# Selective scan: every B product through a transpose, four of them as a matmul with a diagonal of B, sums as transposes, softplus in three ScalarE steps

## What is computed

```
x_dbl = einsum('bkdl,kcd->bkcl', xs, x_proj_weight);  dts, Bs, Cs = split(x_dbl)
delta = softplus(einsum('bkrl,kdr->bkdl', dts, dt_projs_weight) + dt_projs_bias)
def step(h, (u, d, B, C)):
    h = exp(d[..., None] * A) * h + d[..., None] * B[:, :, None, :] * u[..., None]
    y = sum(h * C[:, :, None, :], axis=-1)
out_y = ys + xs * Ds;   y = out_y of the four directions, turned back and added
```

## Time and profile before

| | |
|---|---|
| median of 3 launches | 27518.19 us (27503.76 to 27527.82) |
| the profiled execution | 27545.74 us, span of its core 27544.1 us |
| busy over the span | PE 92%, DVE 85%, ACT 77%, POOL 77% |
| granted TensorE clock, mean | 0.945 |
| bytes moved by DMA | 1243.41 MB, mean 45 GB/s |

### The profile page before, as it was taken

The page is one execution under the profiler, slowest core; times in us unless marked ns, Lnnn a source line. Parts: engine busy times, 40 slices in busy tenths (PEclk is TensorE's granted clock), DMA queues, the critical chain, the costliest instruction groups (busy, mean ns, idle before and its releaser), DMA issues. The chain is left out here.

```text
span 27544.1 us, 304787 instructions
## 1 busy us (share of the span) xinstructions
PE 25272.9 (92%) x87136; PEld 12653.6 (46%) x87136; DVE 23277.2 (85%) x22864; ACT 21119.5 (77%) x39912; POOL 21115.4 (77%) x9545
## 2 busy tenths in 40 slices
PE   7999889998799988999889998899988999889998
PEld 3455444554345544455434554445544455444554
DVE  6799867998679986799867998679986799867998
ACT  4799747997479974799757996579964799747997
POOL 3799737997379973799737997379973799737997
PEclk8999989999899998999989999899998999989999
DMA  0122101221012210122101221012210122101221
GB/s 8 46 64 63 45 8 46 63 63 45 9 46 63 63 45 8 46 63 63 45 8 47 63 63 45 8 48 63 63 46 6 47 63 63 44 8 46 64 63 45
DMA packets 796846, 1243.41 MB, mean 45 GB/s; under 512 B 220800, under 2 KB 238080, under 8 KB 792064
## 3 DMA queue, kind: packets, MB, share of 16 engines
q1 hardware_dynamic: 795136, 1223.32, 15.1%
HBM read 1155.89 MB, written 67.11 MB: 44 GB/s over the span
## 5 line engine op out<-in xcount | busy, mean ns | idle before, releaser
L1590 PE MATMUL ps<-arena,ident 128*128 128x512 f32 x24576 | 11420.8, 596 | 2.8 <-DVE arena L1425 1.8
L1413 DVE TENSOR_TENSOR_SCAN arena<-arena,ps 128x512 f32<-128x512 f32 x7680 | 9250.5, 1259 | 120.2 <-ACT arena L1776 62.7
L1966 POOL TENSOR_TENSOR arena<-arena 128x1536 f32<-128x1536 f32 x1920 | 6636.8, 3462 | 84.6 <-ACT arena L1796 83.8
L1787 ACT ACTIVATE scaled<-arena,cols 128x384 f32<-128x384 f32 x10240 | 5807.5, 606 | 695.8 <-PE ps L1559 695.8
L1590 PEld LDWEIGHTS ps<-arena,ident 128*128 128x128 f32 x24576 | 4350.6, 190 | 4319.9 <-issue 4013.6
L1413 DVE TENSOR_TENSOR_SCAN arena<-ps,arena 128x512 f32<-128x512 f32 x4608 | 5576.4, 1260 | 74.8 <-ACT ps L1776 74.7
L1956 POOL TENSOR_TENSOR arena<-arena 128x1536 f32<-128x1536 f32 x1536 | 5311.3, 3467 | 326.5 <-DVE arena L1413 325.4
L1776 ACT ACTIVATE arena<-arena 128x512 f32<-128x512 f32 x7680 | 5240.8, 713 | 11.6 <-PE ps L1590 11.6
L1559 PEld LDWEIGHTS ps<-ident,scaled 128*128 128x128 f32 x30720 | 3537.4, 141 | 1987.1 <-issue 1173.7
L1559 PE MATMUL ps<-ident,scaled 128*128 128x128 f32 x30720 | 4195.7, 276 | 139.0 <-ACT scaled L1787 60.7
L1776 ACT ACTIVATE ps<-arena 128x512 f32<-128x512 f32 x4608 | 3125.1, 683 | 64.0 <-DVE arena L1413 25.1
(11 more groups left out here) (190 smaller groups left out, 32155.8 us busy)
## 6 DMA issues: line engine op xcount, KB each, us to landing
arena<-rows SPq DMA_DIRECT2D x3456, 256.0 KB, 3.2
spare<-rows SPq DMA_DIRECT2D x640, 256.0 KB, 3.3
arena<-x SPq DMA_DIRECT2D x16, 1536.0 KB, 13.4
x<-arena SPq DMA_DIRECT2D x16, 1536.0 KB, 10.7
arena<-x SPq DMA_DIRECT2D x64, 384.0 KB, 8.0
out<-arena SPq DMA_DIRECT2D x64, 384.0 KB, 3.0
rows<-xd SPq DMA_DIRECT2D x256, 64.0 KB, 2.7
arena<-L_conv_fc_w SPq DMA_DIRECT2D x16, 576.0 KB, 5.3
```

Of the source, the lines that this page charges most:

```text
L1413: nc.vector.tensor_tensor_scan(flip(states(b, n, t)), flip(decays), flip(adds), carry[:, k, N2 * n + t:N2 * n + t + 1], ALU.mult, ALU.add) ...
L1590: nc.tensor.matmul(m.ps[:, t, :], m.ident[:, :], states(b, n, t), start=False, stop=(n == SUMS[t][-1])).then_inc(at[Y_MM[t]], 1)
L1787: nc.scalar.activation(scaled[:, j, :], turned[:, j, :], ACT.Copy, scale=b_cols[:, b % 2, j, n:n + 1]).then_inc(at["scaled_out"], 1)
L1966: nc.gpsimd.tensor_tensor(out, out, each, ALU.mult).then_inc(at["hp_ready"], 1)
```

## The change

The six plain states go away: all 16 products come by TensorE. For twelve (`SCALED`) the pieces are scaled as before, but 13 of the 48 pieces of a block are scaled on GpSimd (`POOL_PIECES`); there are two buffers of `scaled` and two of `turned`. For four (`DIAGONAL` = 3, 6, 11, 15) ScalarE scales the 128x128 identity by the column of B, and `turn_back` is a real matmul of `turned` with it. VectorE multiplies by C only for states 4, 9 and 15, GpSimd for thirteen. `add_up` becomes four transposes that accumulate, so y arises with tokens on partitions; `lift_y` copies it to SBUF, `turn_y` transposes it back, and the older y is added there. The bias of delta enters as a thirteenth row of the matmul. The softplus is Abs, Exp, Ln(1+x) on ScalarE; VectorE has `rounded` ((w+1)-1, from SBUF to SBUF) and `above` (max(x,0)+l, from PSUM); GpSimd's three steps stay. The weights of the projection are kept for two directions at a time and loaded again during the scan; the DMAs of B's rows go.

```diff
-POOL_C = (0, 1, 3, 4, 6, 7, 9, 11, 12, 13)
-TURNED = (1, 2, 4, 5, 7, 8, 10, 11, 13, 14)
+POOL_C = (0, 1, 2, 3, 5, 6, 7, 8, 10, 11, 12, 13, 14)
+DIAGONAL = (3, 6, 11, 15)
+POOL_PIECES = {1: (2, 3), 2: (3,), 4: (2, 3), 7: (2, 3), 8: (3,), 10: (2, 3), 13: (2, 3), 14: (3,)}
...
-                nc.vector.scalar_tensor_tensor(sp_e, sp_w, 1.0, m.ps[:, AH, :], ALU.subtract,
-                                               ALU.subtract).then_inc(at["sp_dve"], 1)
+                nc.vector.tensor_scalar(sp_e, sp_w, 1.0, 1.0, ALU.add, ALU.subtract).then_inc(at["sp_dve"], 1)
+            def above(b, t):
+                dve.wait_ge(at["sp_act"], 3 * u + 3)
+                nc.vector.scalar_tensor_tensor(delta[:, b % 2, t, :], m.ps[:, AH, :], 0.0, sp_l, ALU.max,
+                                               ALU.add).then_inc(at["sp_dve"], 1)
...
+                if n in DIAGONAL:
+                    for j in range(N4):
+                        ins = nc.tensor.matmul(bank(b, n, t)[:, j * 128:(j + 1) * 128], turned[b % 2][:, j, t * 128:(t + 1) * 128],
+                                               diagonals[no % 2][:, j, :], start=True, stop=True)
...
-                nc.tensor.matmul(m.ps[:, t, :], m.ident[:, :], states(b, n, t), start=False,
-                                 stop=(n == SUMS[t][-1])).then_inc(at[Y_MM[t]], 1)
+                for j in range(N4):
+                    ins = nc.tensor.matmul(m.ps[:, t, j * 128:(j + 1) * 128], states(b, n, t)[:, j * 128:(j + 1) * 128],
+                                           m.ident[:, :], start=(n == SUMS[t][0] and j == 0),
+                                           stop=(n == SUMS[t][-1] and j == N4 - 1), is_transpose=True)
...
+            def diagonal(b, n, j):
+                nc.scalar.activation(diagonals[no % 2][:, j, :], m.ident[:, :], ACT.Copy,
+                                     scale=b_cols[:, b % 2, j, n:n + 1]).then_inc(at["diag_out"], 1)
+            def lift_y(b, t):
+                act.wait_ge(at[Y_MM[t]], NS * (b + 1))
+                nc.scalar.copy(y_turned, m.ps[:, t, :]).then_inc(at["y_up"], 1)
...
+                nc.gpsimd.tensor_scalar(scaled[nth(b, n, SCALED) % 2][:, j, :], turned[b % 2][:, j, :], b_cols[:, b % 2, j, n:n + 1], 1.0,
+                                        ALU.mult, ALU.mult).then_inc(at["scaled_pool"], 1)
...
                 if j == 0:
-                    pool.wait_ge(at["sp_dve"], u + 1)
-                    pool.wait_ge(at["sp_act"], 5 * (u + 1))
-                    ins = nc.gpsimd.tensor_tensor(sp_e, sp_l, sp_e, ALU.subtract)
+                    pool.wait_ge(at["sp_dve"], 2 * u + 1)
+                    ins = nc.gpsimd.tensor_tensor(sp_e, sp_w, sp_e, ALU.subtract)
```

More of the change, by code:

```diff
@@ L1330, in selective_scan @@
     hs = m.take(HS, N2 * T)
-    dbu = m.take(DB, N2 * T)
-    turned = m.take(N4, D2)
+    turned = [m.take(N4, D2) for _ in range(2)]
+    scaled = (m.scaled, m.take(N4, D2))
+    y_turned = m.take(T)
+    diagonals = [m.take(N4, 128) for _ in range(2)]
     assert m.top <= 6 * SLOT, m.top
-    scaled, xd, sp_e = m.scaled, m.xd, m.sp_e
+    xd, sp_e = m.xd, m.sp_e
     m.start(SLOTS)
@@ L1475, in _ @@
                 scan(b, 9, 1)
-                correct(ahead, 1)
+                rounded(ahead, 2)
                 scan(b, 9, 2)
-                times_c(b, 8)
                 scan(b, 10, 0)
+                above(ahead, 2)
                 scan(b, 10, 1)
@@ L1482, in _ @@
                 scan(b, 11, 0)
+                times_c(b, 9)
                 scan(b, 11, 1)
-                times_c(b, 10)
                 scan(b, 11, 2)
-                correct(ahead, 2)
                 scan(b, 12, 0)
@@ L1498, in _ @@
                 scan(b, 15, 2)
-                times_c(b, 14)
+                scan(ahead, 0, 0)
+                scan(ahead, 0, 1)
+                scan(ahead, 0, 2)
         @block.tensor
@@ L1585, in add_up @@
                     return
+                if b and n == SUMS[t][0]:
+                    pe.wait_ge(at["y_out"], N2 * (b - 1) + t + 1)
                 if n in DVE_C:
@@ new lines, in _ @@
+                turn_back(past, 14, 2)
+                add_up(past, 9, 2)
+                rows_of(ahead, 2)
+                add_up(past, 10, 0)
+                turn_back(past, 15, 0)
+                add_up(past, 10, 1)
+                turn_back(past, 15, 1)
+                turn_back(past, 15, 2)
+                add_up(past, 10, 2)
+                add_up(past, 11, 0)
+                turn_back(b, 0, 0)
+                turn_back(b, 0, 1)
+                add_up(past, 11, 1)
+                spread_c(past, 15)
@@ L1624, in _ @@
+                turn_back(b, 4, 0)
+                turn_back(b, 4, 1)
+                add_up(past, 14, 2)
+                spread_c(b, 4)
+                turn_y(past, 1)
+                turn_back(b, 4, 2)
+                add_up(b, 0, 0)
+                add_up(past, 15, 2)
                 turn_back(b, 5, 0)
+                add_up(b, 1, 0)
                 turn_back(b, 5, 1)
                 turn_back(b, 5, 2)
-                spread_c(b, 5)
-                take_old(b, 2)
-                delta_of(ahead, 0)
@@ L1630, in _ @@
-                add_up(b, 1, 1)
-                add_up(b, 0, 2)
-                add_up(b, 1, 0)
+                turn_y(past, 2)
+                add_up(b, 0, 1)
+                delta_of(ahead, 1)
+                add_up(b, 0, 2)
+                turn_back(b, 6, 0)
+                add_up(b, 1, 1)
+                turn_back(b, 6, 1)
+                turn_back(b, 6, 2)
+                add_up(b, 2, 0)
+                turn_back(b, 7, 0)
+                add_up(b, 2, 1)
                 add_up(b, 1, 2)
-                turn_back(b, 7, 0)
+                spread_c(b, 9)
@@ L1845, in _ @@
                 scale(b, 5, 3)
+                softplus(ahead, 0, 0)
+                decay(b, 4, 2)
                 save(b, 3)
+                softplus(ahead, 0, 1)
+                decay(b, 5, 0)
+                decay(b, 5, 1)
+                give_y(past, 1)
+                lift_y(past, 2)
+                softplus(ahead, 0, 2)
+                save(b, 4)
                 decay(b, 5, 2)
+                decay(b, 6, 0)
+                scale(b, 7, 0)
+                scale(b, 7, 1)
                 give_y(past, 2)
-                low_row(ahead)
```

571 lines of the change are left out of this document (285 added, 286 removed).

## The result

The changed kernel takes 28931.03 us (median of 4, 28923.39 to 28960.51) against 27520.49 for the kernel before beside it: ratio 1.0516, 95% interval 1.0502 to 1.0529. It is slower by 1,410 us, 5.5 us for each of the 256 blocks, and it lies above the whole range of the prediction.

A forecast was written before the change was run, and what follows sets the result against it. VectorE was taken as the bound, TensorE and GpSimd a step behind. Period 65.0 + 2.6 + 0.1 = 67.7, 0.85 less than today: -218 over 256 blocks, +16 at sample ends, 27.5 off for the median: 27,320, range 26,700 to 27,800.

The forecast's parts named there:

- today's idle: VectorE's 0.3 us of idle time in a block of the kernel before, added to 64.7 of work to give 65.0.
- So work alone would give a period near 65.1: Block period without new waits, set by ScalarE and VectorE together: 3.4 us a block less, 880 us in all.
- one wait that the new order brings: VectorE's `rounded`, SBUF to SBUF, waits for GpSimd's running operation: 2.6 us a block, at the third `rounded`.
- Its own sign of being wrong: VectorE gaps ended by ScalarE would mean dearer diagonals, forecast at 0.29 to 0.385 us each.
- ACT or PE holding it at 66.0 to 67.0: In-between case: ScalarE or TensorE sets the block period at 66.0 to 67.0 us, total 26,870 to 27,120; chance 0.07.
- the case of one held `rounded`: Main case: one contended `rounded` a block, period 67.0 to 68.3 us, total 27,120 to 27,460; chance 0.40.
- The wait predicted: Third `rounded` issued 0.7 us behind GpSimd's `times_c` of state 7, held 2.6; first and second free or nearly.
- The work: Engine loads forecast per block: VectorE 64.7, GpSimd 63.9, ScalarE 65.1, TensorE 61 to 63 us.
- Uncontended, 26,650 to 26,870: Rival: the SBUF path is never contended or the third `rounded` just gets in; period 65.1 to 66.0 us; chance 0.20.
- Slower, the missed gap: Rival: each `rounded` waits for GpSimd's long operations, two or three times a block; 27,670 to 28,160; chance 0.30 for more waits.
- The clock: Rival: transposes do not hold TensorE's clock up, 360 a block take twice as long; period 100, some 35,600; chance 0.03.
- the argument against it: Against the clock rival: at the scan's start TensorE did transposes and a bf16 matmul, and behind them the clock was 1.00.

The follow-up runs named there:

- e1: Changed kernel with `spread_c(past, 15)` moved on TensorE ahead of the last three `turn_back` of its block: 27780.99 us, ratio 1.0094.
- e5: Changed kernel with `high(ahead)` and `keep_rows(ahead)` moved on ScalarE behind `decay(b, 0, 2)`, the spread left late: 28129.13 us, ratio 1.0214.
- e4: Changed kernel with the edits of both e1 and e2: 27001.31 us, ratio 0.9807.
- e10: e4 with `spread_c` and `turn_back` of state 15 ahead of `rows_of` and `add_up(past, 10, 0)`, and GpSimd's `scale(b, 14, 3)` ahead of `times_c(b, 10)`: 26895.04 us.
- e2: Changed kernel with GpSimd's first softplus step of the third tile put ahead of `times_c` of state 7: 28108.06 us, ratio 1.0211.
- e3: Changed kernel with `rounded` reading PSUM in place of SBUF, so the softplus correction's values are wrong: 27918.27 us, ratio 1.0140.

## Why the prediction was wrong

The forecast was 27,320, the result 28,931. The step that failed is the one after "Sum 68.2 - 4.9 + 1.4 = 64.7, with today's idle 65.0" and "So work alone would give a period near 65.1". It carries VectorE's 0.3 us of idle time over from the old order into a new one. The prediction lists what stands in VectorE's row and on GpSimd beside it, but for TensorE and ScalarE it counts work alone. It says "one wait that the new order brings"; there were two, and the one left out was the dearer. Its own sign of being wrong, VectorE gaps ended by ScalarE, came true, but it had put dearer diagonals there, and these last 0.394, close to the 0.385 of its row.

- *The wait left out.* `spread_c(past, 15)` to `high` to decays to scans: VectorE's idle time is 5.82 in place of 0.3. e1 takes 4.49 of it away by moving one matmul, 1,150 us; e5 shows the copy's place on ScalarE to be the link. No rival named it; "ACT or PE holding it at 66.0 to 67.0" had 0.07 and counted work only.
- *With that wait mended the forecast is still missed.* e1 has the hold and not the late spread: period 69.57 where 67.7 was forecast, 27,781 where the case of one held `rounded` had 27,120 to 27,460. Of the 1.87, 1.03 is idle time of VectorE (0.92 of its 1.33 for a decay ahead of scan(15, 0)), 0.62 the three `rounded`, 0.22 other instructions. ScalarE waits 4.34 us a block for TensorE's sums there and 0.93 in e4. So "today's idle" was wrong for the rest of the order too, by 1 us.
- *The wait predicted.* The third `rounded` was to take 0.46 + 2.6 = 3.1: it took 3.28. That GpSimd's `times_c` of state 7 would hold it was right, but it began only 0.23 us ahead of it (2044.79 and 2045.02) where 0.7 was forecast; the third softplus step on GpSimd takes 1.50 (2043.29 to 2044.79) where 1.23 was put. The first was to be free and is (0.40). The second was to be free or nearly so and takes 0.96, so it was 0.5 too low. Sum of the three: 4.6 against 4.0.
- *The work.* Right where the runs can show it. e4 without the held operation has VectorE at 66.38 - 1.27 = 65.1 busy with 1.75 in the three `rounded` (64.7 with 1.4 was predicted), ScalarE at 64.6 (65.1) and GpSimd at 486.23/500 of 66.38 = 64.6 (63.9). The GpSimd piece took 0.59, the predicted length. Diagonal products at full clock: sixteen from 2071.63 to 2073.42, 0.112 each (0.109 to 0.128).
- *Uncontended, 26,650 to 26,870.* e10, with both faults mended and one piece moved, comes to 26,895, 25 us above the rival's range, reached only by changes that it did not know to be needed, and with the second `rounded` still held (0.95).
- *Slower, the missed gap.* The right side, but not the mechanism: no `rounded` was held by two operations of GpSimd in a row.
- *The clock.* The rival did not come: in e2, e3 and e4 the granted clock of the window is 1.00 with the same 360 transposes a block. But the argument against it misread its rows. In the window of the earlier trace rows TensorE did nothing (x0), so its 1.00 says nothing of transposes; in the next window of the kernel before, TensorE works and the clock is low again:

```profile
976.00:980.00 4.00, 2.68 (x7) 1.67 (x8) 3.79 (x4) 4.00 (x8) 1.40 (x1) 0.62 0.28 82
```

  What the rows there could not tell, e4 shows. From 2076.11 to 2085.84 its TensorE does transposes alone, with two pauses of 0.43 and 0.79 us, and the granted clock is 1.00 through it and behind it (1.00 in the windows from 2076 to 2092, two of them here):

```profile
2080.00:2084.00 4.00, 3.98 (x37) 3.74 (x36) 4.00 (x4) 4.00 (x11) 4.00 (x3) 1.00 0.20 66
2084.00:2088.00 4.00, 3.21 (x19) 1.91 (x18) 4.00 (x4) 4.00 (x10) 4.00 (x3) 1.00 0.29 68
```

  So the small chance that the clock got was right, but its reason was not a reason. What the clock does in a kernel of transposes alone no run shows. It was 0.97 in the changed kernel and in e1 and e5, all of which keep the hold (below).

Reconciled per block: 74.19 less 67.7 is 6.49; of it VectorE's idle time 5.52, the three `rounded` 0.64 and the other instructions 0.33. The forecast's base of 68.55 was one block; the mean of the kernel before is 68.75.

## What to carry to other kernels

Sum up the work to find the bound, but when an order is rewritten, write down for every buffer that is used again its last reader and its next writer, with what stands behind that writer on its engine: here one matmul of 0.4 us, put behind 5.3 us of others, starved an engine that does not read its result in that place. A VectorE tensor_scalar from SBUF to SBUF that is issued while GpSimd runs an operation ended about 0.28 us behind that operation here; give it its input in PSUM (0.67 us, never held), or put GpSimd's wait for it ahead of GpSimd's long operation, and look what that delays on GpSimd. When all engines fall below full at once, look for the copy that waits, not for dearer work, and after mending one order check which engine takes the gap over.

## What was not expected of the hardware

A held VectorE operation also cost clock. Windows of the changed kernel around the third `rounded` (2045.02 to 2048.53), columns as above:

```profile
2042.00:2046.00 4.00, 3.49 (x32) 3.25 (x31) 4.00 (x4) 3.98 (x8) 4.00 (x5) 1.00 0.19 66
2046.00:2050.00 4.00, 0.75 (x6) 0.52 (x5) 4.00 (x3) 3.26 (x6) 3.51 (x2) 0.92 0.09 33
2050.00:2054.00 4.00, 3.94 (x18) 3.54 (x18) 4.00 (x5) 0.09 (x1) 2.39 (x3) 0.50 0.10 33
2054.00:2058.00 4.00, 4.00 (x31) 3.94 (x30) 3.57 (x3) 3.65 (x9) 4.00 (x2) 0.72 0.00 0
```

The scans stand behind the held operation, `turn_back` behind the scans, and TensorE, which waits 3.25 us for a scan, has 0.75 us of work in four. Behind that pause its granted clock is 0.50, which is 1.2 of 2.4 GHz, and it returns some microseconds later. While it is low TensorE does 18 instructions in 3.94 us, and ScalarE waits for its sums (0.09 busy). Avoiding the hold saved 3.33 us a block (e2) where the operation shrank by 2.88; of the other 0.45, VectorE's idle time gives 0.22 and its other instructions 0.23. Whether the clock is behind these is not shown. In e2, which keeps the late spread and loses the hold, the window's clock stayed at 1.00.
